# Turning the next tile's z between the two halves of the experts' second layer

## What is computed

```python
def _L1_ffn_ref(x, W1, b1, W2, b2, Wr, br):      # E, D, H = 8, 256, 1024
    routing_probs = jax.nn.softmax(x @ Wr + br, axis=-1)
    indices = jnp.argmax(routing_probs, axis=-1)
    out = jnp.zeros_like(x)
    for i in range(8):
        mask = (indices == i).astype(x.dtype)[..., None]
        xi = x * mask
        h = jax.nn.relu(xi @ W1[i] + b1[i])
        out = out + (h @ W2[i] + b2[i])
    return out
...
x = x + _L1_ffn_ref(_layernorm(x, axis=-1), ...)
```

## Time and profile before

| | us |
|---|---|
| median of 3 runs | 1664.19 |
| lowest and highest run | 1663.76, 1664.63 |
| the profiled execution | 1662.31 |
| its span, first to last instruction | 1660.6 |
| stretch of the experts' tiles, from the first turning on | 1357.0 to the end |

### The profile page before, as it was taken

The page is one execution under the profiler, slowest core; times in us unless marked ns, Lnnn a source line. Parts: engine busy times, 40 slices in busy tenths (PEclk is TensorE's granted clock), DMA queues, the critical chain, the costliest instruction groups (busy, mean ns, idle before and its releaser), DMA issues. The chain is left out here.

```text
span 1660.6 us, 35783 instructions
## 1 busy us (share of the span) xinstructions
PE 1414.4 (85%) x11323; PEld 1195.4 (72%) x11323; DVE 1276.8 (77%) x2223; ACT 1008.6 (61%) x2527; POOL 438.7 (26%) x638
## 2 busy tenths in 40 slices
PE   3899999879985019789999999999999649989897
PEld 2455555558863019789998888989898539988897
DVE  6988888766869897657777777777777579978786
ACT  2466656545559636366667666766666318867675
POOL 3211111100000000212232222222222256667666
PEclk9999999979999559899999999999999769999999
DMA  5311011000024103510111111111101057111110
GB/s 194 121 57 31 28 32 28 27 1 0 1 66 136 38 0 112 156 76 24 33 33 50 35 32 32 36 40 32 32 29 33 27 222 299 44 44 43 45 47 16
DMA packets 66241, 96.75 MB, mean 58 GB/s; under 512 B 10214, under 2 KB 57327, under 8 KB 63346
## 3 DMA queue, kind: packets, MB, share of 16 engines
q1 hardware_dynamic: 60546, 83.16, 15.3%
q0 software_dynamic: 5616, 12.60, 2.4%
HBM read 76.57 MB, written 21.90 MB: 59 GB/s over the span
## 5 line engine op out<-in xcount | busy, mean ns | idle before, releaser
L1668 ACT ACTIVATE c_w_raw<-c_ps_score,c_shift 128x128 f32<-128x128 f32 x512 | 184.7, 398 | 133.1 <-DVE c_shift L1520 125.1
L2061 PE MATMUL d_ps_hT<-d_zT,d_w_tile 128*128 128x128 f32 x1248 | 148.3, 278 | 2.1 <-DVE d_zT L2166 2.1
L2061 PEld LDWEIGHTS d_ps_hT<-d_zT,d_w_tile 128*128 128x128 f32 x1248 | 145.2, 195 | 2.7 <-DVE d_zT L2166 2.7
L805 PE MATMUL b_ps<-b_down_high,b_inner 128*128 128x256 f32 x384 | 71.0, 289 | 87.8 <-DVE b_inner L1087 87.8
L362 PE MATMUL a_ps_score<-a_keys,a_qT 128*128 128x512 f32 x256 | 137.1, 618 | 3.9 <-ACT a_qT L552 2.2
L2232 ACT ACTIVATE d_h<-d_ps_hT,d_b1T 128x128 f32<-128x128 f32 x312 | 88.7, 367 | 64.8 <-PE d_ps_hT L2061 63.8
L2074 PE MATMUL d_ps_y<-d_w_parts,d_hT 128*128 128x256 f32 x936 | 124.4, 290 | 1.8 <-DVE d_res L2193 1.8
L805 PEld LDWEIGHTS b_ps<-b_down_high,b_inner 128*128 128x128 f32 x384 | 60.7, 194 | 88.1 <-issue 88.1
L1668 ACT ACTIVATION_READ_ACCUMULATOR c_w_raw<-c_ps_score,c_shift 128x1 f32 x512 | 121.1, 237 | 0.0
L2185 DVE TENSOR_TENSOR d_w_parts<-d_w,d_w_parts 128x1024 fp32r<-128x1024 f32 x78 | 95.8, 1229 | 31.4 <-ACT d_w_parts L2244 27.2
L2074 PEld LDWEIGHTS d_ps_y<-d_w_parts,d_hT 128*128 128x128 f32 x936 | 117.2, 195 | 2.4 <-DVE d_res L2193 2.0
(11 more groups left out here) (260 smaller groups left out, 3743.1 us busy)
## 6 DMA issues: line engine op xcount, KB each, us to landing
d_w<-w_in SPq DMA_DIRECT2D x16, 1024.0 KB, 10.2
b_x_space<-w_in SPq DMA_DIRECT2D x16, 512.0 KB, 3.6
a_x<-x_in SPq DMA_DIRECT2D x4, 1024.0 KB, 7.6
a_keys<-ctx_blocks_in SPq DMA_DIRECT2D x128, 32.0 KB, 2.1
a_v_raw<-ctx_in SPq DMA_DIRECT2D x4, 1024.0 KB, 8.3
x_scratch<-a_x SPq DMA_DIRECT2D x32, 128.0 KB, 1.7
b_x_space<-x_scratch SPq DMA_DIRECT2D x32, 128.0 KB, 2.5
x_scratch<-b_x_space SPq DMA_DIRECT2D x32, 128.0 KB, 1.9
```

What stands on the lines that cost most here:

```text
L805: last = pe.matmul(ps[:, t, 0:D], inner[:, s, a, f, t * P:(t + 1) * P], down_parts[b][:, f, :], start=(j == 0), stop=(j == NF * len(PARTS) ...
L1668: last = act.activation(prob[:, n, j, :], ps_score[:, n % 2, j, :], ACT.Exp, scale=float(KD) ** -0.5, bias=shift[:, n, j:j + 1], accum_out ...
L2061: last = pe.matmul(ps_hT[:, f, :], w1_tile[:, half, k, n * P:(n + 1) * P], zT[:, s, k, :], start=(k == 0), stop=(k == ND - 1))
```

## The change

The second layer is split into a call for each half. The turning of the next tile's z, which stood ahead of the whole second layer of the previous tile, now stands between its two halves. The wait for the result buffer (`y_read`) stays ahead of the first half. Where there is no second layer (step 0) the order is as before.

```diff
-                def second_layer(j, s):
-                    if inside(j, 1, NT - 1):
+                def second_layer(j, s, half):
+                    if half == 0 and inside(j, 1, NT - 1):
                         pe.wait_ge(y_read, j)
-                    for half in range(2):
-                        pe.wait_ge(hT_ready, 2 * j + half + 1)
-                        pe.wait_ge(w2_ready, 2 * j + half + 1)
-                        for n, (a, b) in product(range(FB // 2), PARTS):
-                            f = FB // 2 * half + n
-                            last = pe.matmul(ps_y[:, 0:D], hT[:, s, a, f, :], w2_parts[:, half, b, n, :],
-                                             start=(f == 0 and (a, b) == PARTS[0]), stop=(f == FB - 1 and (a, b) == PARTS[-1]))
-                        last.then_inc(w2_used, 1)
+                    pe.wait_ge(hT_ready, 2 * j + half + 1)
+                    pe.wait_ge(w2_ready, 2 * j + half + 1)
+                    for n, (a, b) in product(range(FB // 2), PARTS):
+                        f = FB // 2 * half + n
+                        last = pe.matmul(ps_y[:, 0:D], hT[:, s, a, f, :], w2_parts[:, half, b, n, :],
+                                         start=(f == 0 and (a, b) == PARTS[0]), stop=(f == FB - 1 and (a, b) == PARTS[-1]))
+                    last.then_inc(w2_used, 1)
 
                 def step(j, s, i):
                     if inside(j, 0, NT - 1):
                         first_layer(j, s)
+                    if inside(j, 1, NT):
+                        second_layer(j - 1, (s + NS - 1) % NS, 0)
                     if inside(j, 0, NT - 2):
                         turn_z(j + 1, (s + 1) % NS, i + (s == NS - 1))
                     if inside(j, 1, NT):
-                        second_layer(j - 1, (s + NS - 1) % NS)
+                        second_layer(j - 1, (s + NS - 1) % NS, 1)
```

## The result

The changed kernel takes 1648.8 us (median of four runs, 1645.16 to 1652.59), the kernel before beside it 1663.97 (four runs, 1662.92 to 1664.63). The ratio is 0.991 with a 95% interval of 0.9886 to 0.9933: 15.2 us less. The forecast was 14 us less and 1650.

What follows compares the result with a forecast made beforehand. The prediction took GpSimd's 7.82 us round to bound the later part of the experts' stage. 22 tiles falling from 7.83 to 7.25 us (12.8 us) plus 1.3 us at the end made 14 us: 1650 us, range 1640 to 1666.

Steps and rivals of the forecast that it cites:

- the second part: Experts' stage from 1443.0 to 1630.8: GpSimd never idle, its 7.82 us round sets the tile; TensorE misses 21.4 us.
- a late tile: Tile whose z gather is late, timed from its turning; at least 6.8 us, longer if z's issue loses to the second subtraction.
- the forecast's third kind: Tile after a 7.66 us one: scatter meets first subtraction, index copy the second, z goes at 5.4; 8.3 us.
- rival 3: Scatter issue later than 1.5 us after the turning hits the first subtraction; 8.4 us rounds, 1667 to 1675 us; chance 0.14.
- The forecast's cycle: Repeating tiles behind tile 15's turning: 6.8, 7.35, 7.66 and 8.3 us kinds, 44.2 us for 6.1 tiles, 7.25 us each.
- the share of races won: GpSimd's issue of z starting close to VectorE's second subtraction: 7 won, 5 lost, taken from the earlier trace.
- The end: Behind tile 37's turning: 12 multiplications less, at most 1.47 us, of which 1.3 us taken as gain.
- First part and switch: Experts' stage up to 1443, and the extra boundary between kinds of multiplication: cost 0, at most 1.4 us over 14 tiles.
- the forecast's two terms: 12.8 us less over 22 tiles up to tile 37's turning, plus 1.3 us less behind it; together 14 us.
- Rival 1: GpSimd's rounds stay at 7.82 us; TensorE gains 1.47 us once, not per tile; 1662.7 us; chance 0.18 together with Rival 4.
- Rival 2: TensorE becomes the bound throughout, the race always won; 27 us less, 1637 us; chance 0.08.
- Rival 4: Second layer's first half itself waits for hT or w2; same time as Rival 1, chance 0.18 together with it.

Runs made afterwards that it cites:

- nocopy_before: Kernel before, with GpSimd's loop written out and its three index copies per tile removed, so each indirect DMA reads ids directly; 1635.07 us.
- pool_sooner: Kernel before, with GpSimd's loop written out and the always-met wait for ids between each index copy and its issue removed; 1630.12 us.
- unrolled_after: Changed kernel with only GpSimd's loop written out for all 39 tiles, index copies kept; 1647.63 us.
- dve_later: Changed kernel plus one small VectorE copy per tile ahead of the second subtraction of w2; 1631.9 us.
- before_dve_later: Kernel before plus one small VectorE copy per tile ahead of the second subtraction of w2; 1632.45 us.
- turn_quarter: Changed kernel with the turning of z placed after 6 of the second layer's 24 multiplications instead of 12; 1659.85 us.
- pool_later: Changed kernel with GpSimd's copy of z's indices made twice, so that the issue of z starts later; 1664.13 us.
- nocopy_after: Changed kernel with GpSimd's loop written out and its three index copies per tile removed, indirect DMAs reading ids directly; 1646.81 us.
- pool_sooner_after: Changed kernel with GpSimd's loop written out and the always-met wait for ids between each index copy and its issue removed; 1630.03 us.

## Why the prediction was right, and where its steps were off

**The bound.** That GpSimd's round bounds the second part was read from the earlier trace rows and held: *nocopy_before* and *pool_sooner* shorten that round alone, and TensorE's waits for the gather of z are gone.

**The frame of a late tile.** The forecast set a late tile out against its turning: copy of z at 0.5, first subtraction 1.45, second at 3.4 to 3.5. The timeline of a late tile of the changed kernel, turning at 1464.99:

```profile
1464.99 0.44 PE L2049 MATMUL d_ps_zT<-ident,d_z 128*128 128x128 f32 x2 [0.72 <-DMA d_z<-z_scratch,d_z_ids]
...
1465.57 0.42 DVE L2167 COPY d_zT<-d_ps_zT 128x256 f32<-128x256 f32 x1 [0.72 <-PE d_ps_zT L2049]
...
1466.54 1.22 DVE L2186 TENSOR_TENSOR d_w_parts<-d_w,d_w_parts 128x1024 fp32r<-128x1024 f32 x1
...
1466.76 1.91 POOL L2005 DMA_INDIRECT out<-d_res,d_out_ids  x1 [0.81 <-issue]
...
1468.57 1.22 DVE L2186 TENSOR_TENSOR d_w_parts<-d_w,d_w_parts 128x1024 fp32r<-128x1024 f32 x1
1468.67 1.16 POOL L1975 COPY d_z_ids<-d_ids 128x1 int32 x1
...
1470.62 1.07 POOL L1979 DMA_INDIRECT d_z<-z_scratch,d_z_ids  x1 [0.79 <-POOL d_z_ids L1975]
...
1473.07 0.44 PE L2049 MATMUL d_ps_zT<-ident,d_z 128*128 128x128 f32 x2 [1.22 <-DMA d_z<-z_scratch,d_z_ids]
```

Measured from the turning these are 0.58, 1.55 and 3.58. The tile itself is the forecast's third kind: the scatter meets the first subtraction (1.91 us), the index copy the second (1.16 us instead of 0.19), z goes at 5.63, and the next turning comes 8.08 us after this one; 8.3 was forecast. The scatter starts 1.77 us after the turning, past the 1.5 us that rival 3 named. The next tile is of the same kind (8.38 us, scatter at 1.64), which the forecast did not have; in the one behind it the scatter starts at 1.20, ahead of the subtraction, and the chain of rival 3 breaks off.

**The subtraction no longer waits for ScalarE.** So it was forecast. VectorE's list of waits from 1369 to 1640, first of before, then of after:

```profile
DVE d_w_parts L2185 <- ACT d_w_parts L2244: 26.2, 33, 2.0
```

```profile
DVE d_w_parts L2186 <- ACT d_w_parts L2245: 4.5, 17, 0.3
```

**The prices of the tiles were right, their shares were not.** Of the 22 tiles in the second part 8 took 6.65 to 6.95 us, 4 took 7.20 to 7.40, 5 took 7.56 to 7.77 and 5 took 8.08 to 8.58. The forecast's cycle, scaled to 22 tiles, has 12.2 of 6.8, 2.6 of 7.35, 3.6 of 7.66 and 3.6 of 8.3. With the forecast's prices and the measured counts the sum is 8 x 6.8 + 4 x 7.35 + 5 x 7.66 + 5 x 8.3 = 163.6 us, against 162.86 measured. One term that was mis-sized is the share of races won, taken from before as 7 to 5 (one of the five lost is an issue of x3, at 1583.05; of z's issues that started with a subtraction or behind it 7 were won and 4 lost). In the changed kernel's trace 16 issues of z met the second subtraction's start, 7 won and 9 lost. In the forecast's own cycle this share gives 2 + 7/9 = 2.78 tiles of 6.8, one of 7.66, one of 8.3 and 9/7 of 7.35 us: 44.3 us for 6.06 tiles, 7.31 us instead of 7.25. That is 1.2 us of the 3.5 between the forecast 12.8 and the measured 9.3. The rest lies in what follows a lost race: two tiles of 8.1 to 8.6 us in a row, twice, where the cycle has one, and 7.56 and 7.61 us for the second of two lost races in a row, where it has 7.35.

The share does not belong to the order of the instructions. *unrolled_after* has the same order, and its profiled execution (1647.75 us) won 12 races and lost 7: there the 22 tiles take 158.61 us, 7.21 each, and TensorE waits 9.8 us for z, as forecast (7.25 and about 10). The changed kernel's only trace is that of its slowest execution, so what its median execution won is not known.

GpSimd and VectorE at a lost race, one lost by less, and a won one:

```profile
1484.80 1.22 DVE L2186 TENSOR_TENSOR d_w_parts<-d_w,d_w_parts 128x1024 fp32r<-128x1024 f32 x1
1484.92 2.04 POOL L1979 DMA_INDIRECT d_z<-z_scratch,d_z_ids  x1 [0.79 <-DVE d_res L2197]
...
1492.35 1.22 DVE L2186 TENSOR_TENSOR d_w_parts<-d_w,d_w_parts 128x1024 fp32r<-128x1024 f32 x1
1492.38 2.13 POOL L1979 DMA_INDIRECT d_z<-z_scratch,d_z_ids  x1 [0.79 <-POOL d_z_ids L1975]
...
1499.78 1.26 DVE L2186 TENSOR_TENSOR d_w_parts<-d_w,d_w_parts 128x1024 fp32r<-128x1024 f32 x1
1499.78 1.07 POOL L1979 DMA_INDIRECT d_z<-z_scratch,d_z_ids  x1 [0.78 <-POOL d_z_ids L1975]
```

The pair at 1492.35 has the 0.03 us that won in the earlier trace rows, and lost. A share read from 12 such pairs was a weak term. The Trainium skill, "SBUF — State Buffer", section "Who interferes with whom", infers that a tensor_tensor does not hold up the making of a GpSimd DMA's descriptors; in these rows, as in the earlier trace rows, one holds up an indirect DMA. The same section says that a VectorE instruction with two SBUF inputs contends with a GpSimd instruction that reads SBUF, and the indices of these indirect DMAs lie there; no run tells which of the two parts of an issue is held up. That by this page only VectorE's copies would hold up an issue, as the prediction has it, follows from the inference alone and leaves out this other half.

**The other half of the mechanism was not in the forecast.** It told the gain by z's operations and the scatter's, and x3's were left out. GpSimd's time over the 22 tiles from tile 15's turning to tile 37's, added up by line from the two timelines (an operation that runs across an edge is counted up to it):

| GpSimd, us in 22 tiles | before | after | difference |
|---|---|---|---|
| copy of z's indices | 11.1 | 11.6 | +0.5 |
| issue of z | 32.2 | 32.8 | +0.6 |
| copy of x3's indices | 14.1 | 7.9 | -6.3 |
| issue of x3 | 31.2 | 24.5 | -6.7 |
| copy of the scatter's indices | 7.7 | 4.7 | -3.0 |
| issue of the scatter | 23.2 | 28.8 | +5.6 |
| pauses | 52.6 | 52.6 | 0.0 |
| sum | 172.2 | 162.9 | -9.3 |

So GpSimd is never idle but for its pauses in either kernel, and the gain is not in z's issue at all: x3's copy and issue, and the scatter's copy, are held up less, the scatter's issue more. x3's issue and copy in the groups by line from 1458 to 1618 (count, busy us, mean ns; idle before), first of before, then of after:

```profile
L1992 POOL DMA_INDIRECT d_x<-x_scratch,d_x_ids x21 | 30.2, 1437 | 16.3 <-POOL d_x_ids L1988 15.5 <-DVE d_res L2196 0.8
...
L1988 POOL COPY d_x_ids<-d_ids 128x1 int32 x20 | 12.6, 629 | 0.1
```

```profile
L1992 POOL DMA_INDIRECT d_x<-x_scratch,d_x_ids x22 | 25.3, 1150 | 17.1 <-POOL d_x_ids L1988 17.1
...
L1988 POOL COPY d_x_ids<-d_ids 128x1 int32 x21 | 7.4, 353 | 0.1
```

In the new order both subtractions stand some 2 us earlier against the turning (1.4 to 1.9 and 3.3 to 4.0 us after it, mostly 3.3 to 3.4 and 5.2 to 5.4 before), so that x3's copy mostly comes behind them. *dve_later* and *before_dve_later* show that, with pauses of 0.79 us, the race of x3 decides whether GpSimd keeps step at all; *pool_sooner*, with 0.27, keeps step without winning it.

**The end.** Forecast was 1.3 us less behind the turning of tile 37; it became 0.9 us more. TensorE's last multiplication does end 0.5 us nearer to that turning (22.37 us behind it, 22.83 before), less than forecast, as the first tile takes 1627.90 - 1620.26 = 7.64 us with 0.77 us of waiting, against 6.73 without in before. But the forecast put TensorE and VectorE at the end of the last chain, and there stands GpSimd's backlog. Its last issue of x3, first of before, then of after:

```profile
1650.66 1.06 POOL L1992 DMA_INDIRECT d_x<-x_scratch,d_x_ids  x1 [3.30 <-issue]
```

```profile
1640.94 1.07 POOL L1992 DMA_INDIRECT d_x<-x_scratch,d_x_ids  x1 [3.30 <-issue]
```

It starts 19.82 us behind tile 37's turning before and 20.68 after, and each kernel ends 9.9 us later, with the last three scatters one behind the other.

**First part and switch**: forecast 0; 6.66 us a tile from tile 2's turning to tile 14's, against 6.67 before, to tile 13's. The 1.4 us that tile 2's turning lost at the start is the counterpart of the 12 multiplications saved at the end, and the forecast counted only the second.

Measured, the forecast's two terms make 9.3 - 0.9 = 8.4 us of the 14, and the profiled pair gives 9.7. The medians give 15.2, as this profiled execution is the slowest of the four after and that of before is below its own median. So the forecast time is met closer than its terms are, and in part by luck: by the profiled pair it was 4 us too hopeful.

**The rivals.** Rival 1 (only 1.5 us, once) falls: the gain is spread over 22 tiles, and *turn_quarter* is not in proportion. Rival 2's 1637 us is not reached by the change; the kernels that keep GpSimd in step go below it, to 1630 to 1632. Rival 3's chain exists, in 5 of 22 tiles, and in *pool_later*, where with the lost races it undoes the gain. Rival 4 falls with the waits: none for hT or w2 is listed on TensorE.

## What to carry to other kernels

When several small operations of an engine with a low busy share form a round for each tile, add its busy time and its pauses over the stage, not over the page: a round longer than the tile is the bound at any share. If close starts against another engine decide that round's length, reorderings elsewhere move the time in either direction by how the starts fall, and a share of won races from a dozen pairs does not carry over to the new order, nor from one program of that order to another (7 of 16 and 12 of 19 here). Shorten the round itself first: here a wait that was always met cost 0.5 us three times a tile, and without it the place of the turning no longer mattered.

## What was not expected of the hardware

- One more VectorE copy of 0.19 us in each tile made the kernel before 31 us faster (1663.3 to 1632.45 us), as GpSimd's issue of x3 then starts with the subtraction or up to 0.17 us ahead of it (from 1387.8 to 1601.3).
- A start 0.03 us behind the subtraction goes both ways: 1.07 us in the earlier trace rows, 2.13 us at 1492.38.
- VectorE's copy of z starts 0.47 to 0.69 us after the turning in the changed kernel, and up to 1.8 us after it, with VectorE idle, where the indirect DMAs read ids directly and z's is being issued during the turning (*nocopy_after*). TensorE's signal itself is late there (0.96 to 1.78 us instead of 0.39 to 0.45). The cause is open.
- A wait on a semaphore that is always met, between GpSimd's copy and its issue, makes the pause there 0.79 us instead of 0.27 (*pool_sooner_after* beside *unrolled_after*, which has 0.78).
